# First attention: query and key rows restacked through DRAM by DMA instead of by products with selection matrices

## The reference

```
x = x + attn(layernorm(x))
qkv = x @ w_qkv + b_qkv                      # [512, 768] for a sequence
scores = einsum('bhqd,bhkd->bhqk', q, k) * HEAD_DIM ** (-0.5)     # HEAD_DIM = 16
scores = where(mask, -inf, scores)           # diff < 0, and for local heads diff > WINDOW
w = softmax(scores);  ctx = einsum('bhqk,bhkd->bhqd', w, v)
out = ctx @ w_out + b_out
```

## Time and profile before

| | |
|---|---|
| median of 3 runs | 2841.06 us (2840.2 to 2847.95) |
| profiled execution | 2840.67 us, its span 2838.9 us |
| busy share of the span | PE 87%, PEld 69%, DVE 68%, ACT 57%, POOL 48% |
| mean granted TensorE clock | 0.953 |
| first attention | about 0 to 950 us |

### The profile page before, as it was taken

One profiled execution on the slowest core, in us unless ns is written; L12 is line 12 of the kernel. 1 busy time (PEld: TensorE's weight loads), 2 busy tenths in 40 slices (PEclk: granted clock), 3 DMA queues, 4 the chain that ended last, 5 costly groups with the idle time before them and its releaser, 6 DMA issues. The chain is left out here.

```text
span 2838.9 us, 52966 instructions
## 1 busy us (share of the span) xinstructions
PE 2468.8 (87%) x16640; PEld 1962.6 (69%) x16656; DVE 1939.0 (68%) x4957; ACT 1604.4 (57%) x3209; POOL 1373.2 (48%) x1593
## 2 busy tenths in 40 slices
PE   6988899889988688988999599999989579999983
PEld 3666666666666457877999477777767479888862
DVE  7677767776776387686556578888876645666754
ACT  4766666766766225555777345444434257666641
POOL 1333334333433244444754354577777345655566
PEclk9999999999999799998999799999999789999996
DMA  4112111211121336756998433454444378888884
GB/s 167 54 69 83 54 61 54 98 53 54 61 90 46 127 117 212 251 177 209 324 323 307 152 92 104 134 160 151 152 144 154 138 264 306 290 301 302 296 269 146
DMA packets 208230, 464.66 MB, mean 164 GB/s; under 512 B 26834, under 2 KB 118996, under 8 KB 206932
## 3 DMA queue, kind: packets, MB, share of 16 engines
q1 hardware_dynamic: 158804, 326.99, 33.7%
q0 software_dynamic: 49152, 134.28, 14.2%
HBM read 217.37 MB, written 243.27 MB: 162 GB/s over the span
## 5 line engine op out<-in xcount | busy, mean ns | idle before, releaser
L374 POOL TENSOR_SCALAR_AFFINE_SELECT a_pt<-a_pt 128x512 f32<-128x512 f32 (+1 forms) x320 | 173.9, 543 | 597.1 <-ACT a_pt L481 596.9
L1051 POOL DMA_INDIRECT slots<-f_xn,k_picks x256 | 262.6, 1026 | 241.5 <-PE f_Z L1559 90.8
L2640 POOL DMA_INDIRECT f_yg<-made,k_picks x256 | 254.9, 996 | 171.3 <-PE f_Z L2833 97.2
L622 DVE TENSOR_REDUCE a_mx<-a_FB 128x2 f32<-128x384 f32 (+4 forms) x512 | 274.5, 591 | 52.7 <-PE a_FB L747 37.0
L481 ACT ACTIVATE a_pt<-a_S 128x384 f32<-128x384 f32 (+3 forms) x640 | 254.7, 456 | 76.8 <-PE a_S L769 76.4
L1779 POOL DMA_INDIRECT k_yg<-made,k_picks x224 | 225.0, 1005 | 128.1 <-issue 61.1
L741 PE MATMUL a_FB<-a_kb,a_qb 128*128 128x192 bf16 (+4 forms) x1008 | 193.5, 255 | 69.1 <-issue 40.5
L1789 POOL DMA_INDIRECT slots<-b_staged,k_picks x192 | 194.9, 1015 | 78.3 <-issue 57.9
L741 PEld LDWEIGHTS a_FB<-a_kb,a_qb 128*128 128x128 bf16 x1024 | 98.9, 97 | 136.2 <-issue 68.2
L463 ACT ACTIVATE a_qb<-a_qh,a_headmask 128x512 bf16<-128x512 f32 x256 | 182.9, 731 | 0.0
L2765 DVE SCALAR_TENSOR_TENSOR f_cb<-f_yg,k_wall,f_cb 128x256 f32<-128x256 f32 x256 | 124.1, 485 | 85.9 <-DMA f_yg<-made,k_picks 78.8
(11 more groups left out here) (415 smaller groups left out, 6720.1 us busy)
## 6 DMA issues: line engine op xcount, KB each, us to landing
f_xg<-slots SPq DMA_DIRECT2D x164, 512.0 KB, 6.0
made<-f_ye SPq DMA_DIRECT2D x164, 512.0 KB, 4.1
slots<-a_zeros SPq DMA_DIRECT2D x16, 2560.0 KB, 9.2
a_xin<-in_x SPq DMA_DIRECT2D x16, 512.0 KB, 10.0
x_after_a<-a_xres SPq DMA_DIRECT2D x16, 512.0 KB, 2.9
f_wexp<-in_w_exp SPq DMA_DIRECT2D x8, 1024.0 KB, 11.7
normalised<-b_rxn SPq DMA_DIRECT2D x16, 512.0 KB, 3.6
f_xs<-normalised SPq DMA_DIRECT2D x16, 512.0 KB, 5.7
```

What stands on the lines that cost most here:

```text
L374: ins = nc.gpsimd.affine_select(out=v[:, :, 0:P], in_=v[:, :, 0:P], compare_op=ALU.is_ge, fill=0.0, base=0, pattern=[[0, nh], [1, P]], cha ...
L622: nc.vector.tensor_reduce(mx[:, heads[0]:heads[0] + nh, qb], src[:, 0:nh * n].rearrange("p (h c) -> p h c", c=n), AX.X, ALU.max).then_inc( ...
L1051: nc.gpsimd.indirect_dma_start(out=slots[GROUP1[s]][:, :], out_offset=bass.IndirectOffsetOnAxis(ap=picks[:, i:i + 1], axis=0), in_=xn[:, s ...
L2640: nc.gpsimd.indirect_dma_start(out=yg[:, b, k, :], out_offset=None, in_=made[s // BATCH][:, :], in_offset=bass.IndirectOffsetOnAxis(ap=pic ...
```

## The change

The selection products, their copies and the selection matrices are gone. Instead, when the high and low parts of q and k of one half (8 heads) are made, SyncE writes these four tiles of 128 x 512 numbers to four scratch tensors in DRAM (`spill`, 256 KB each), and when they have landed it reads them back into the stacked rows of `ks` and `qs` (`stack`, nine transfers for a half: for each of three groups of rows one into 32 partitions of `ks` and two into 16 partitions each of `qs`). In a sequence that is 8 spills and 18 stacks. The factor of the scores (DH ** -0.5) moves into the weights of q. The zeros of `qs` are written once, at the start, by VectorE. The first scores of a half wait for its nine transfers (u0 for `stacked[0]`, u12 for `stacked[1]`).

```diff
-    for p, slot in enumerate((15, 15, 16, 16, 18, 18, 21, 22)):
-        timed += [(slot, ("rk", p)), (slot, ("rq", p))]
...
+                def spill(s, t):
+                    at_least(sp, stacked[t], STACK * s)
+                    at_least(sp, f_dve, ev(s, NF, at["k", t]))
+                    for i, part in enumerate((kh, kl, qh, ql)):
+                        sp.dma_start(turned[i][t * P:(t + 1) * P, :], part[:, t, :].bitcast(F32)).then_inc(spilled[t], 16)
+
+                def stack(s, t):
+                    at_least(sp, s_done, ev(s - 1, 2 * NU, 2 * t_last[2 * t + 1] + 1))
+                    at_least(sp, spilled[t], SPILL * (s + 1))
+                    for i, (k, q) in enumerate(((0, 2), (0, 3), (1, 2))):
+                        r = i * PAIR
+                        sp.dma_start(ks[r:r + PAIR, t * PT:(t + 1) * PT, :].bitcast(F32),
+                                     turned[k][t * P:(t + 1) * P, :].rearrange("(a c) n -> c a n", c=PAIR)
+                                     ).then_inc(stacked[t], 16)
+                        for j in range(2):
+                            sp.dma_start(qs[r + j * DH:r + (j + 1) * DH, t * HT + j:(t + 1) * HT:2, :].bitcast(F32),
+                                         turned[q][t * P:(t + 1) * P, :].rearrange("(a j d) n -> j d a n", j=2, d=DH)[j]
+                                         ).then_inc(stacked[t], 16)
...
                     if core:
+                        stack(s, 1)
                         m_rows(s, 1)
                     if tail:
                         at_least(sp, t_dve, summed)
                         sp.dma_start(rows, xres[:, 1 - par]).then_inc(x_stored, 16)
                         at_least(sp, x_stored, stored)
                     if front:
+                        if s < 0:
+                            sp.wait_ge(dve_ready, 2)
+                        spill(s + 1, 0)
+                        spill(s + 1, 1)
+                        stack(s + 1, 0)
                         m_rows(s + 1, 0)
                         clear(s + 1)
...
-                        at_least(act, f_done, ev(s - 1, NF, NF - 1))
+                        at_least(act, spilled[k], SPILL * s)
+                        if kind == "k":
+                            at_least(act, k_half, ev(s - 1, QT, k))
...
-                    elif kind == "rk":
-                        at_least(act, s_done, ev(s - 1, 2 * NU, 2 * t_last[k // 2] + 1))
-                        nc.scalar.copy(ks[0:ONES, k, :], src[0:ONES]).then_inc(f_act, 1)
...
+                            nc.scalar.activation(wraw[:, :, 0:H], wraw[:, :, 0:H], ACT.Copy, scale=DH ** -0.5).then_inc(w_scaled, 1)
...
-                            for name, parts in (("kh", (1, 1, 0)), ("kl", (0, 0, 1)), ("qh", (1, 0, 1)), ("ql", (0, 1, 0))):
-                                for i, used in enumerate(parts):
-                                    nc.vector.tensor_copy(sel[name][:, :, i], sel0[:, :, i] if used else selz[:]).then_inc(dve_ready, 1)
...
-                nc.vector.memset(selz[:], 0.0).then_inc(dve_ready, 1)
-
+                nc.vector.memset(qs[0:ONES].bitcast(F32), 0.0).then_inc(dve_ready, 1)
                 nc.vector.memset(ks[ONES:ONES + 1].bitcast(F32), 1.0).then_inc(dve_ready, 1)
...
-                    elif kind in ("rk", "rq"):
...
-                        pe.matmul(dst[0:ONES, :], sel[c + "h"][:, a].rearrange("p b c -> p (b c)"), hi[:, t, :],
-                                  start=True, stop=False)
-                        ins = pe.matmul(dst[0:ONES, :], sel[c + "l"][:, a].rearrange("p b c -> p (b c)"), lo[:, t, :],
-                                        start=False, stop=True)
...
                     if u == t_first[t]:
-                        by = [i for i in range(NF) if FRONT[i][0] in ("rk", "rq") and FRONT[i][1] // 2 == t]
-                        at_least(pe, f_act, ev(s, NFA, act_no[[i for i in by if by_act[i]][-1]]))
-                        if not all(by_act[i] for i in by):
-                            at_least(pe, f_dve, ev(s, NFD, dve_no[[i for i in by if not by_act[i]][-1]]))
+                        pe.wait_ge(stacked[t // 2], STACK * (s + 1))
```

More of the change, by code:

```diff
@@ L177, in phase_a @@
     s_bank, s_before = rotation(2 * NU, 3)
[L178 to L181, removed]
     at = {use: i for i, use in enumerate(FRONT)}
@@ L259, in phase_a @@
         f_done = sem("f_done")
-        f_act = sem("f_act")
+        w_scaled = sem("w_scaled")
+        spilled, stacked = ([sem(n + "%d" % i) for i in range(QT)] for n in ("spilled", "stacked"))
         f_dve = sem("f_dve")
@@ L292, in phase_a @@
         W_DMAS = 16 * (4 + 2 * QT)
+        SPILL, STACK = 16 * 4, 16 * 9
         mt_at = [FRONT.index(("mT", g)) for g in range(2)]
@@ L314, in m_rows @@
                     last = 2 * t_last[0] + 1 if g == 0 else 2 * NU - 1
-                    made = in_register(sp, ev(s, NFD, dve_no[mt_at[g]]))
+                    made = in_register(sp, ev(s, NF, mt_at[g]))
                     used = in_register(sp, ev(s - 1, 2 * NU, last))
@@ L436, in front_use @@
                     kind, k = FRONT[i]
-                    if kind in ("T", "q", "k", "rk", "rq") and not (kind == "rq" and not by_act[i]):
+                    if kind in ("T", "q", "k"):
                         at_least(act, f_done, ev(s, NF, i))
@@ L445, in front_use @@
                         dst, b = (qh, bq) if kind == "q" else (kh, bk)
-                        at_least(act, f_done, ev(s - 1, NF, NF - 1))
+                        at_least(act, spilled[k], SPILL * s)
+                        if kind == "k":
+                            at_least(act, k_half, ev(s - 1, QT, k))
                         nc.scalar.activation(dst[:, k, :], src, ACT.Identity, bias=b[:, k:k + 1]).then_inc(hi_done, 1)
-                    elif kind == "rk":
-                        at_least(act, s_done, ev(s - 1, 2 * NU, 2 * t_last[k // 2] + 1))
-                        nc.scalar.copy(ks[0:ONES, k, :], src[0:ONES]).then_inc(f_act, 1)
-                    elif kind == "rq" and by_act[i]:
-                        at_least(act, s_done, ev(s - 1, 2 * NU, 2 * t_last[k // 2] + 1))
-                        for j in range(2):
-                            ins = nc.scalar.activation(qs[0:ONES, 2 * k + j, :], src[0:ONES], ACT.Copy,
-                                                       scale=pairmask[0:ONES, j:j + 1])
-                        ins.then_inc(f_act, 1)
                 def mask_q(s, h):
@@ L601, in front_use @@
                     at_least(dve, f_done, ev(s, NF, i))
-                    if kind == "rq":
-                        at_least(dve, s_done, ev(s - 1, 2 * NU, 2 * t_last[k // 2] + 1))
-                        for j in range(2):
-                            ins = nc.vector.tensor_scalar(qs[0:ONES, 2 * k + j, :], src[0:ONES],
-                                                          pairmask[0:ONES, j:j + 1], None, ALU.mult)
-                        ins.then_inc(f_dve, 1)
-                        return
                     if kind == "v":
@@ L834, in body @@
                             fronts()
[L836 removed]
+                pe.wait_ge(w_ready, 12)
                 iterations(pe, body)
@@ L2884, in transformer_block @@
     made1 = [t[0:n * STEP * P, :] for t, n in zip(made[NG - 1:] + made[:NG - 1], STEPS1)]
-    phase_a(nc, x, x1, slots, w["w_qkv"], w["b_qkv"], w["w_out"], w["b_out"], nseq)
+    turned = [nc.dram_tensor("turned%d" % i, (H, SEQ), F32, kind="Internal").ap() for i in range(4)]
+    phase_a(nc, x, x1, slots, turned, w["w_qkv"], w["b_qkv"], w["w_out"], w["b_out"], nseq)
     with ExitStack() as ctx:
```

49 lines of the change are left out of this document (15 added, 34 removed).

## The result

The changed kernel takes 2703.51 us (median of 4 runs, 2696.9 to 2707.77); the kernel before, measured beside it, 2844.51 us (2840.2 to 2852.16). The ratio is 0.9499 with a 95% interval of 0.9467 to 0.9532: faster by 5%, 141 us. The forecast was 2690 us, 2645 to 2745. The profiled execution took 2696.9 us, 143.8 less than the profiled one of before.

The account below looks back on a forecast made before the run. The prediction took TensorE to set the pace, busy 51.46 of 57.33 us per sequence. From 2840.7 us it took 163 over 16 sequences, added 4 for the start and 8 for the first sequence: 2690 us, range 2645 to 2745.

Parts of the forecast that it names:

- D: Sequence's last stretch, after the global maxima's transposes to the next first scores unit: from 17.22 to 9.2 us (8.1 to 11.4).
- A: Sequence's first stretch, u0 (first scores unit) into u4: from 11.21 to 9.0 us (7.9 to 9.1).
- rival 3: A and D go down to their floors, every wait in them gone: 2654 us, chance 0.10.
- rival 1: In A and D waits only change their name, to maxima and masks; only products go: 2725 us, chance 0.17 (to 2745).
- The products alone: TensorE's 32 removed selection products per sequence: 5.82 us in D and 2.15 us in A.
- nothing of their own: Price of VectorE's ten and ScalarE's fourteen removed copies per sequence, said to lie beside TensorE's work.
- The waits behind the masks: Two TensorE waits of 1.23 us in D, for head masks behind ScalarE's copies: both gone, 2.46 us.
- Hidden transfers: Steady-state spills and stacks cost 0 us, the first nine stacks landing 8 us before the next u0.
- the calendar: SyncE's schedule per sequence: spills issued from 22.8 us, stacks from 28 to 33.4, landed at 39, next u0 at 47.1.
- Rival 2: Stacks land late at u0 because SyncE's queue takes transfers one after the other: 2941 us, chance 0.12.
- The first sequence: Second-half stacks and local minima row queue behind 8.5 MB of zeros; wait at u8 of 8 us (4 to 16).
- The start: VectorE's one-time clear of qs before its first statistics: 4 us added (2 to 7).

Follow-up runs that it names:

- the dummies: The late zeros kernel with 32 products of 96x512 per sequence put back on TensorE, results overwritten, without the copies that followed: 2785.02 us.
- wide rows: The late zeros kernel with the 18 stacks reading the same bytes into 128 and 64 partitions of a spare tile, scores from constant ks and qs: 2687.04 us.
- late zeros: The changed kernel with the first sequence's 6144 KB of zeros issued in the last sequence instead: 2689.22 us, ratio 0.9466.

## Why the prediction was right, and where it was not

- **The bound, and D and A.** TensorE sets the pace, and the products and the waits around them are what was saved: 11.07 us of 57.34, forecast 10.2 (8.0 to 12.4). D came to 8.18 us, almost TensorE's floor of 8.1 (rival 3), and not 9.2. A fell by 1.76, less than its lower end of 2.1 (11.21 - 9.1), which let only the products go: there the waits changed their name, as rival 1 had it, from 0.66, 0.46 and 0.19 us to 0.97 and 0.88. With the 0.5 us left in D the waits for maxima add up to 2.3 us, under the 3 that the prediction had set as rival 1's sign.
- **The shares inside.** The products alone are worth 5.86 us, not 7.97, since 1.5 us of waits run beside them and the dummies take 7.4 us of TensorE, and ScalarE's copies not "nothing of their own" but 0.60 us beside the products. The waits behind the masks were read rightly: 2.86 us of the period hang on ScalarE's standing for the products, forecast 2.46 for the two in D.
- **Hidden transfers.** Right in the sum, wrong in the margin: 2.0 to 4.1 us to spare in all sequences but one, not 8. Two steps of the calendar failed. SyncE waits 2.5 us for its store to land ahead of the spills, and "5.4 us at the clear's rate" for the time from the last issue to landing was 8.8 in the sequence shown (379.91 to 388.7). The Trainium skill, SBUF — State Buffer, section "Door 1: The DMA port swizzle", gave an estimated 11.7 us for the nine. They took 11.3 to 13.4, and 9.6 instead of 12.5 with wide rows, so the trace agrees with that rule as far as this test goes.
- **Rival 2** did not come: the nine overlap, 13.3 us in place of its 35. With the zeros ahead of the stacks its lateness did come, by another cause: the loop was 2 to 4 us away from it.
- **The first sequence** is the step that failed: 19.19 us instead of 8. The zeros were in at 71.9, about as forecast (73); the stacks behind them took 14.5 us instead of 5.4, and u8 was due at 67.4 rather than 69.6. The lower clock behind the wait cost 2.6 us more. The late zeros took back 17.5 us. The prediction's rate for the stacks was that of the clear, from 128 partitions into DRAM, and no row had their shape.
- **The start:** 5.3 us, forecast 4 (2 to 7).
- **The sum.** At the first product of the phase behind the attention the changed kernel is ahead by 154.4 us (828.5 against 982.9); the terms of the forecast gave 151. That 154.4 and 151 are so close is luck in part: the loop gave 14 us more than forecast (16 x 0.87), and the first sequence cost 14 us more (19.19 + 2.6 - 8). From that first product to the last one of the routed experts it takes 1770.1 us, 10.0 more than before; in the profiled execution (2696.9) this is more than the whole distance to 2690, and the median lies 6.6 us above that execution. The forecast had no term for untouched phases. Chance alone is unlikely to be their cause (1760.1 and 1761.2 before, 1763.2 to 1779.6 in twelve kernels with the change or parts of it); half of the 10 us lies in the first phase, where the granted clock is lower for the same instructions. Why a change in the attention moves the clock behind it stays open.

## What to carry to other kernels

When work leaves the engine that sets the pace, price the chain around it and not only its instructions: products, copies that wait for them and masks behind the copies were each worth another amount together than alone. Price a transfer by a row with the same shape on both sides: a rate from 128 partitions is no rate into 16. And when a queue that only filled a table gets work that someone waits for, look at the first pass, where the old bulk may stand ahead of the new.

## What was not expected of the hardware

- The DMA engines were fully busy (share 1.09) while the last stacks moved 153 GB/s, and just as busy (0.99) at 397 GB/s behind them: here the busy share told nothing about the rate.
- VectorE's TENSOR_SCALAR on 128x4 numbers took 6.12 us instead of 0.17 while GpSimd cleared `qs`, and ended as that did (13.1 us); the additions ahead of it took 0.16 us under the same clear. The Trainium skill, SBUF — State Buffer, section "Who interferes with whom", says that some of VectorE's operations share a port pair with GpSimd and that the later one stands still until the other ends. The trace agrees.
- TensorE's granted clock fell to 0.50 for some 3 us behind the same two waits (0.97 and 0.88 us), in some sequences and not in others of the same kernel, which makes a period 47.8 us instead of 46.27. With the clock behind the attention it is a likely reason why runs of one kernel lie apart (2678.09 to 2703.43 us for the late zeros); that is not shown, since one trace of each was kept. What decides it stays open.
